# One step of the build moved a round later: the f16 remainder of x, on VectorE and on ScalarE

## The reference, cut to what matters

```python
def sage_conv(x, src, dst, W_l, b_l, W_r, n_nodes):
    msg = x[src]
    agg = segment_sum(msg, dst, n_nodes)
    cnt = segment_sum(ones, dst, n_nodes)
    return (agg / maximum(cnt, 1)) @ W_l.T + b_l + x @ W_r.T
# L0: out = sage_conv(relu(sage_conv(x))), x = layernorm(x + out)
# L1: three layers of
#   m = concat([x[dst], x[src], edge_attr]) @ W.T + b
#   relu(segment_sum(m, dst)), the first two followed by batchnorm and relu
# result: layernorm(x + L1(x))
```

## Time and profile before

| | us |
|---|---|
| median of 3 runs (1163.93 to 1168.71) | 1168.71 |
| the profiled execution, its own time | 1165.03 |
| the span of its trace, first to last instruction | 1162.2 |
| TensorE matmul busy | 972.3 (84%) |
| VectorE busy | 727.4 (63%) |
| ScalarE busy | 395.5 (34%) |
| GpSimd busy | 128.0 (11%) |
| mean granted TensorE clock, of full speed | 0.928 |

### The profile page before, as it was taken

How to read it: one execution, slowest core, us unless ns; L and a number is a source line. 1 busy time by engine, 2 the same in 40 slices (tenths; PEclk the granted TensorE clock), 3 DMA queues, 4 the chain that set the end, 5 groups by cost and what they waited for, 6 DMA issues and landing times. The chain is left out here.

```text
span 1162.2 us, 19469 instructions
## 1 busy us (share of the span) xinstructions
PE 972.3 (84%) x7567; PEld 581.9 (50%) x7567; DVE 727.4 (63%) x1415; ACT 395.5 (34%) x808; POOL 128.0 (11%) x150
## 2 busy tenths in 40 slices
PE   0247868878677867999999999998999998999993
PEld 0246767768566754455555444444434443444441
DVE  5797999999999943623433755544464554334434
ACT  1484788787877740200000110113320204210000
POOL 4121313323222220000000000000000000000001
PEclk9768988889888997999999999998999998999996
DMA  6325456555445339983674526665036755037740
GB/s 163 62 71 196 176 169 202 194 180 184 149 143 164 122 126 275 424 281 129 271 318 175 222 89 266 244 246 222 14 124 236 279 207 222 19 144 285 284 164 23
DMA packets 67304, 216.80 MB, mean 187 GB/s; under 512 B 32176, under 2 KB 45227, under 8 KB 53667
## 3 DMA queue, kind: packets, MB, share of 16 engines
q1 hardware_dynamic: 59188, 164.52, 39.7%
q0 software_dynamic: 8016, 50.95, 12.1%
HBM read 170.69 MB, written 44.74 MB: 185 GB/s over the span
## 5 line engine op out<-in xcount | busy, mean ns | idle before, releaser
L1380 PE MATMUL PM<-Aring,Xop 128*128 128x512 fp8e4 (+1 forms) x1960 | 398.7, 363 | 0.0
L1380 PEld LDWEIGHTS PM<-Aring,Xop 128*128 128x128 f16 x1960 | 181.5, 98 | 217.6 <-issue 17.3
L820 PE MATMUL PW<-Aring 128*128 128x52 fp8e4 (+3 forms) x2151 | 121.2, 220 | 79.8 <-ACT F L886 77.7
L820 PEld LDWEIGHTS PW<-Aring 128*128 128x128 fp8e4 x2151 | 114.7, 105 | 84.1 <-ACT F L886 80.4
L1905 ACT ACTIVATE F<-PH,bag 64x512 f32<-64x512 f32 (+1 forms) x39 | 25.5, 658 | 372.0 <-PE PH L1599 371.9
L1380 PE MATMUL PM<-Ares,Xop 128*128 128x512 fp8e4 x588 | 137.1, 388 | 2.8 <-ACT Xop L1944 1.4
L1738 DVE TENSOR_SCALAR S<-PM 128x256 f32<-128x256 f32 (+1 forms) x75 | 31.4, 418 | 112.8 <-PE PM L1380 96.0
L1380 PEld LDWEIGHTS PM<-Ares,Xop 128*128 128x128 f16 x588 | 56.0, 99 | 71.1 <-issue 8.5
L886 ACT ACTIVATE F<-PW 128x392 uint16<-128x392 f32 x196 | 84.5, 511 | 11.4 <-PE PW L820 10.3
L1529 POOL DMA_DIRECT2D out<-dd x12 | 9.1, 757 | 703.7 <-DVE dd L1700 703.7
L678 DVE TENSOR_TENSOR Aring<-Ares 128x4096 uint16<-128x4096 uint16 x31 | 70.8, 2284 | 6.0 <-PE PW L820 5.6
(11 more groups left out here) (158 smaller groups left out, 1204.4 us busy)
## 6 DMA issues: line engine op xcount, KB each, us to landing
Aring<-adj SPq DMA_DIRECT2D x72, 1568.0 KB, 9.8
adj<-Aring POOLq DMA_DIRECT2D x12, 1568.0 KB, 6.4
adj<-Xop POOLq DMA_DIRECT2D x12, 1568.0 KB
Ares<-adj SPq DMA_DIRECT2D x6, 1568.0 KB, 21.5
rc<-ea_sum SPq DMA_DIRECT2D x36, 128.0 KB, 5.5
eaf<-in_erow SPq DMA_DIRECT2D x62, 51.0 KB, 1.9
Aring<-adj SPq DMA_DIRECT2D x4, 784.0 KB, 4.4
rc<-rc_d SPq DMA_DIRECT2D x12, 256.0 KB, 9.5
```

The lines of the kernel that those rows point to most:

```text
L820: last = nc.tensor.matmul(PW[begun % RING][:, c:c + 52 * (z - y)].rearrange("p (d v b) -> p d v b", d=z - y, b=2), lo[:, h % 2, i, :].bitc ...
L1380: last = nc.tensor.matmul(o, x[:, h, :], rhs, start=h == 0, stop=h == NT - 1)
```

## The change

The subtraction on VectorE (line 744) moves from behind `large(0)` to behind `large(1)`: `small(1)` and `large(1)` now come ahead of it, `attributes(0)` and `digits(2)` still follow it. The scaling on ScalarE (line 971) moves from the end of round 1, behind `table(3)`, to the end of round 2, behind `across(2)` and `natural(4)`. No instruction is added or removed, and no semaphore's count changes.

```diff
             for h in range(NH):
                 t = h // 2
                 large(h)
-                if h == 0:
+                if h == 1:
                     v.wait_ge(s_xh, 1)
                     nc.vector.tensor_tensor(scratch(m["Xop"][1]), m["R"][:], m["Xop"][0][:, :, 0:64],
                                             ALU.subtract).then_inc(s_xd, 1)
...
                 if h % 2 and h // 2 + 3 < TS:
                     table(h // 2 + 3)
-                if h == 1:
+                if h == 2:
                     act.wait_ge(s_xd, 1)
                     nc.scalar.mul(m["Xop"][0][:, :, 64:128], scratch(m["Xop"][1]), LO).then_inc(s_xl, 1)
                 if h >= 1:
```

## The result

The changed kernel takes 1161.22 us in the median of 20 runs (1158.87 to 1164.24), the kernel before 1167.33 us (1163.93 to 1168.87, also 20). The ratio is 0.9951, with a 95% interval of 0.9943 to 0.9959: 5.7 us faster, at the edge of what counts here as no change (0.5%). Two repetitions gave 0.9965 (0.9954 to 0.9977) and 0.9958 (0.9943 to 0.9973), so the mean of the three is 0.9958, or 4.9 us. The forecast said 1163 us in a range of 1157 to 1168.5, and −3.8 us.

The account below looks back on a forecast made before the run. The prediction took VectorE to bound the build and TensorE the layers. From 1165.03 us, 6.5 gained and 2.7 lost gave 1161.2 us, or 1164.9 on the median's level; it forecast the middle, 1163 us, range 1157 to 1168.5.

Parts of the forecast that it names:

- The bound: In the build VectorE is the bound, so idle time removed there comes off the kernel's end unless another wait swallows it.
- The first term: VectorE in the build: the 6.25 us wait before the subtraction and 0.23 us before L720 go, 6.5 us gained.
- The margin of 1.8 us at L744: At the moved subtraction: ScalarE's rounding L945 ends at 42.19 us, 1.8 us before VectorE wants it at 44.0.
- rival 4: At the moved subtraction: `large(1)` is over before ScalarE's rounding ends, so part of the wait stays; chance under 0.01.
- The second term: ScalarE, end of round 2: the scaling delays `high(3)` and the evacuations, so VectorE loses 2.7 us by `unpack(1)`.
- the 0.60 us wait: VectorE's wait before `unpack(1)` for the 13th evacuation at 79.65 us, taken to show there is no slack.
- The clock: TensorE's clock over the product of stage 1: taken as 0, between 2.6 us gained and 2.9 us lost.
- The sum: Whole kernel: 1165.03 − 6.5 + 2.7 = 1161.2 us, or 1164.9 on the runs' median; a change of −3.8 us.
- rival 1: The whole wait is gained, or the clock adds to it: −6.5 us, 1158.5 us (1162 on the median's level); chance 0.2.
- Rivals 2 and 3: Later TensorE wait swallows the gain, 1164.1 us, chance 0.16; low clock over several products makes it slower, +2.0 us, 0.05.
- The level: Whole kernel's time: profiled execution or runs' median as base, giving 1161.2 or 1164.9 us; the middle, 1163, was forecast.

Follow-up runs that it names:

- VectorE's half: The kernel before with only the subtraction moved behind `large(1)`, the scaling left at the end of round 1: ratio 0.9949, median 1158.71 us.

## Why the prediction was right, and what was mis-sized

**The bound.** Right, to within 2.8 us. What VectorE lost or won by round 4 it kept: from the start of `large(6)` to the end of the span the traces of before took 1053.1 and 1055.6 us, those of the changed kernel 1054.2, 1055.7 and 1055.8, and those of the other edits 1054.0 to 1055.9. These differences follow no edit: the two traces of before alone differ by 2.5.

**The first term, 6.5 us gained.** The mechanism is shown three times over: keep the wait and the gain is gone, remove it on ScalarE's side and it is there without the change, do both and it doesn't double. The size was the mistake. It was read from one execution as 6.25 us, and the bounds put around it (6.25 to 6.6) held only what follows the wait. The prediction followed the wait back to L945 and not to the gather behind it; its line "no wait is on a DMA" is true of VectorE's own list alone. The wait is a difference of two chains, VectorE's `large(0)` and that gather, and the distances in the eleven traces put it at 6.25 to 8.3, on average 7.4. The trace in hand had the smallest. The four kernels that have the gain without the loss bear the size out: their ratios (0.9949, 0.9927, 0.9936, 0.9935) have a mean of 0.9937, 7.4 us below the kernel before. A wait for a transfer should have had a range from the spread of the other transfers of its kind.

**The margin of 1.8 us at L744**, on which rival 4 rested, was for the same reason too wide: 42.40 against an end of L945 at 41.89 leaves 0.5 in the first trace after. When L945 ended latest, 11.3 and 11.7 us behind the start of `large(0)`, it was 0.2 and 0.0, and VectorE waited 0.34 and 0.48 us for `high(0)`. In the six traces with the moved subtraction behind the gather the margin was 1.5 to 0.0 us, so rival 4's chance of under 0.01 was too small, though it came true in none.

**The second term, 2.7 us lost.** Right on average: 2.5 to 2.8 us between the changed kernel and VectorE's half, 1.93 us of it in front of L720 of chunk 3 (forecast 1.9), the rest mostly in front of `unpack(1)` (0.73 to 1.12 us, where the half alone has 0.33 and some 1.3 was forecast), and twice as much for twice the work. But the 0.60 us wait that the prediction took as the sign of no slack isn't always there: the second trace of before has none in front of `unpack(1)`. TensorE's 53 matmuls ahead of it took 3.89 us in that trace and 4.82 in the first. Against one or the other the changed kernel loses 2.2 to 2.6 or 2.8 to 3.2 us from `large(3)` to `large(4)`, more than the bound of 2.8 allowed. That L971 cost nothing in its old place holds too: back there it gives the time of the best.

**The clock.** Taken as 0, with −2.6 and +2.9 as ends. The product of stage 1 took 8.15 us in the trace that the forecast used and 7.3 to 7.8 in all twelve others, and from `large(4)` to `large(6)` it was 27.70 us there against 26.89 to 27.39. So the first trace of before was 0.3 to 0.8 us slow here, and 0.7 of the 5.6 us between the two first spans is that. It isn't the change's: the second trace of before shows 7.31 us and 26.89. The slow product is also the one behind the longest idle time, 6.91 us where the others have 5.6: TensorE had run the 56 matmuls of round 3 in 3.10 us, which took 4.40 in the second trace of before, and so stood idle sooner. That idle time makes the product slower is not shown, since only one trace has it. The Trainium skill, page "TensorE: Matmul & The Clock Gate", Part 1, says that the number of slow matmuls differs between executions of one kernel. The twelve products behind the same idle time bear it out, with 7.31 to 7.80 us; with the thirteenth the spread is 0.8 us, not the 5.5 between the forecast's two ends.

**The sum.** 7.4 + 0.2 − 2.6 = 5.0 us against 4.9 measured in the mean of three; the forecast's −3.8 lacked 1.1, all in the first term. The first measurement, −5.7 us, is nearer to rival 1's −6.5 than to −3.8, so the time alone would have spoken for the rival. But rival 1's reason is refuted: the loss at the scaling is there. What it described is got by VectorE's half alone or by the scaling two calls earlier, 5.9 and 8.5 us by their ratios (0.9949 and 0.9927). Rivals 2 and 3, a slower clock over the products, showed in no trace.

**The level.** The forecast saw two values in the runs before and took the middle of two sums, which stands for a level of 1166.9 us. Twenty runs fill 1163.93 to 1168.87 with no gap over 1.3 us, and their median is 1167.33. That 1163 came so close to 1161.22 is in part this choice, for which the prediction had no reason. The 3.7 us between the profiled execution and the median of three are what executions of one kernel differ by: the two traces of before differ by 1.1 us from `large(0)` to `large(4)`, by 0.8 the other way from there to `large(6)`, and by 2.5 behind it. The first is the gather's, less 0.7 us of the wait in front of `unpack(1)`; for the last no cause is shown.

## What to carry to other kernels

Before a step is moved past a wait, look in the queue of each engine that it touches for the next wait there: the same instruction is free ahead of it and costs its full time behind it. A change of two engines' orders is two changes, and here, by the traces, one gave 7.6 us and the other took 2.6 back. And a wait that ends with a transfer should be sized from several executions, since one trace gives one draw of it.

## What the runs showed of the hardware

While GpSimd subtracted two SBUF tiles (6.13 us), VectorE's next instruction with two SBUF operands took 5.93 us instead of 0.20. The Trainium skill, page "SBUF — State Buffer", section "Who interferes with whom", describes a port pair that the two share and that one holds for the whole of an instruction. The two ends, 49.40 and 49.34 us, agree with that. So does the kernel before, in small: six of its 59 instructions of L712 took 0.75 to 1.31 us instead of 0.20, and each of the six ended 0.05 to 0.06 us behind an addition on GpSimd (L584, 33x256). One other, of 0.19 us, began 0.02 us behind such an addition and was not held; the one behind it (L715) was, with 1.09 us instead of 0.69. GpSimd needed 6.13 us where VectorE needs 3.42, so idle time of GpSimd was no cover for this work.
